# Routing tokens of three chunks inside the attention stream, into fixed slot regions per expert

## What is computed

```python
scores = x_flat @ gate_w + gate_b                       # (2048, 8)
topk_vals, topk_idx = jax.lax.top_k(scores, TOP_K)      # TOP_K = 2
topk_probs = jax.nn.softmax(topk_vals, axis=-1)
combine_w = zeros((T, N_EXPERTS)).at[tok, topk_idx].add(topk_probs)
h = relu(einsum('td,edf->etf', x_flat, w1) + b1[:, None, :])
y = einsum('etf,efd->etd', h, w2) + b2[:, None, :]
out = einsum('te,etd->td', combine_w, y)
x = _layernorm(x + out)
```

## Time and profile before

| | us |
|---|---|
| median of 3 runs | 3154.45 (3149.6 to 3155.65) |
| the profiled execution | 3158.21 |
| its span | 3156.4 |
| TensorE busy, share of the span | 2783.8 (88%) |
| VectorE busy | 2059.6 (65%) |
| ACT busy | 1566.9 (50%) |
| POOL busy | 267.7 (8%) |

### The profile page before, as it was taken

The page is one execution under the profiler, slowest core; times in us unless marked ns, Lnnn a source line. Parts: engine busy times, 40 slices in busy tenths (PEclk is TensorE's granted clock), DMA queues, the critical chain, the costliest instruction groups (busy, mean ns, idle before and its releaser), DMA issues. The chain is left out here.

```text
span 3156.4 us, 85067 instructions
## 1 busy us (share of the span) xinstructions
PE 2783.8 (88%) x35706; PEld 1409.0 (45%) x35707; DVE 2059.6 (65%) x4240; ACT 1566.9 (50%) x2122; POOL 267.7 (8%) x381
## 2 busy tenths in 40 slices
PE   6796978999986988799999999999999999379992
PEld 3574643444443553244344443433333333246661
DVE  4444138888843236688899898989999995412224
ACT  2232213666662222266777776766676778023331
POOL 2113011000010001300000000000000000210003
PEclk9897988999997998699999999999999999589996
DMA  5412032011001004221211221111111110711112
GB/s 157 120 44 94 0 106 79 20 22 39 3 2 37 1 12 131 74 61 45 57 43 41 62 52 37 45 45 55 45 44 45 45 45 2 260 45 32 32 33 88
DMA packets 114940, 173.56 MB, mean 55 GB/s; under 512 B 19946, under 2 KB 90491, under 8 KB 114211
## 3 DMA queue, kind: packets, MB, share of 16 engines
q1 hardware_dynamic: 108772, 160.02, 17.7%
q0 software_dynamic: 5824, 8.49, 0.9%
HBM read 127.63 MB, written 40.51 MB: 53 GB/s over the span
## 5 line engine op out<-in xcount | busy, mean ns | idle before, releaser
L1307 DVE TENSOR_REDUCE d_part_max<-d_ps_m 128x1 f32<-128x512 f32 (+1 forms) x1964 | 1126.9, 630 | 91.0 <-PE d_ps_m L1294 56.7
L1622 ACT ACTIVATE d_prob<-d_ps_s 128x1024 f32<-128x1024 f32 x928 | 898.6, 1021 | 342.8 <-PE d_ps_s L1484 336.3
L1294 PE MATMUL d_ps_m<-k_st,q_st 97*32 97x512 bf16 (+1 forms) x5296 | 480.9, 361 | 22.2 <-DVE d_part_max L1307 18.0
L1484 PE MATMUL d_ps_s<-q_st,k_st 98*32 98x512 bf16 x5104 | 441.1, 382 | 9.7 <-ACT d_prob L1622 8.3
L698 DVE TENSOR_REDUCE x_part_max<-x_att_ps_m 128x1 f32<-128x512 f32 (+2 forms) x578 | 307.6, 585 | 43.4 <-PE x_att_ps_m L683 17.3
L939 ACT ACTIVATE x_att_prob<-x_att_ps_s 128x1024 f32<-128x1024 f32 (+3 forms) x296 | 258.2, 921 | 131.1 <-PE x_att_ps_s L820 78.1
L1294 PEld LDWEIGHTS d_ps_m<-k_st,q_st 97*32 97x32 bf16 x5296 | 143.5, 96 | 279.5 <-DVE d_part_max L1307 130.5
L1502 PE MATMUL d_ps_o<-d_prob,a_values 128*32 128x512 f32 x2048 | 267.1, 595 | 0.0
L1294 PE MATMUL d_ps_m<-q_st 97*32 97x512 bf16 (+1 forms) x2560 | 231.9, 362 | 2.6 <-DVE d_part_max L1307 0.6
L1484 PEld LDWEIGHTS d_ps_s<-q_st,k_st 98*32 98x32 bf16 x5104 | 138.8, 97 | 187.7 <-issue 74.7
L1502 PE MATMUL d_ps_o<-d_prob,x_values 128*32 128x512 f32 x1664 | 215.4, 593 | 0.4 <-ACT d_prob L1622 0.4
(11 more groups left out here) (328 smaller groups left out, 3336.2 us busy)
## 6 DMA issues: line engine op xcount, KB each, us to landing
k_st<-parts_k SPq DMA_DIRECT2D x90, 256.0 KB, 5.6
k_st<-parts_k SPq DMA_DIRECT2D x90, 208.0 KB, 4.7
l_w<-in_l_w SPq DMA_DIRECT2D x16, 1024.0 KB, 13.4
q_st<-parts_q SPq DMA_DIRECT2D x48, 256.0 KB, 5.0
q_st<-parts_q SPq DMA_DIRECT2D x192, 64.0 KB
q_st<-parts_k SPq DMA_DIRECT2D x30, 256.0 KB
q_st<-parts_k SPq DMA_DIRECT2D x30, 208.0 KB
parts_q<-a_proj_parts SPq DMA_DIRECT2D x16, 384.0 KB, 2.5
```

What stands on the lines that cost most here:

```text
L1294: mm = pe.matmul(bank[q:q + COLUMNS, 0:w], self.query(s, h, ROW_MASK + 1, a * P + q, COLUMNS), self.key(s, h, ROW_MASK + 1, k, w), start=T ...
L1307: dve.tensor_reduce(self.part[:, h * QT + a, i:i + 1], bank[:, 0:w], AX.X, ALU.max).then_inc(s_read, 1)
L1484: mm = pe.matmul(ps_s[u][k:k + COLUMNS, hh, :], maxima.key(s, h, ROW_MAX + 1, kt * P + k, COLUMNS), maxima.query(s, h, ROW_MAX + 1, 0, QC) ...
L1622: act.activation(prob[:, p % 2, 2 * u:2 * u + 2, :], ps_s[u][:, :, :], ACT.Exp, scale=scale).then_inc(s_prob, 1)
```

## The change

- `Plan.close_chunks` hangs three tasks on segment 1's chunks 0 to 2: `gate`, `count` and `scatter`, 14, 17 and 19 pairs behind the chunk's end, that is in the second step of the next chunk. `gate` and `count` use banks of the ring.
- `Router` holds what `route` and `place_tokens` did, for one chunk of four token tiles at a time. Expert e owns the slots from e x 2048 on; a running count `seen` goes from chunk to chunk.
- `dispatch` takes the place of `route` and `place_tokens`. It does the last chunk alone (8 scatters) and makes two tables: each loop pass's expert, and `tile_row`, its tile in the slots.
- `x_slots` has 136 tiles, all cleared; results are stored over the tokens' rows, and `y_slots` is gone.
- SP's loads and stores in `expert_ffn` find their rows by `tile_row`.
- SP loads the biases and two experts in `dispatch`; the other six are issued by POOL at the start of `expert_ffn`.

```diff
+SLOT_TILES = E * NT + E
@@ Plan.close_chunks
+            if si == 1 and c < NQ - 1:
+                self.tasks[start + 14].append(("gate", c))
+                self.tasks[start + 17].append(("count", c))
+                self.tasks[start + 19].append(("scatter", c))
@@ Router
+    def logits(self, pe, c, bank, s_logits):
+        for a in range(QT):
+            for m in range(DT):
+                start = (c * QT + a) * P
+                mm = pe.matmul(bank[:, a * E:(a + 1) * E], self.x_fm[:, m, start:start + P], self.w[:, m, :],
+                               start=(m == 0), stop=(m == DT - 1))
+        mm.then_inc(s_logits, 1)
+    def choose(self, dve, link, c, bank, s_taken, s_gates, n):
...
+        link(*(dve.max(self.best[:, a, :], self.logit[:, a, :]) for a in range(QT)))
+        link(*(dve.max_index(self.index[:, a, :], self.best[:, a, :], self.logit[:, a, :]) for a in range(QT)))
...
+    def counts(self, pe, bank, s_counts):
+        flat = self.gates[:, :, :, :].rearrange("p a s e -> p (a s e)")
+        pe.matmul(bank[:, 0:2 * self.LOGITS], self.ones[:, :], flat, start=True, stop=True)
+        pe.matmul(bank[:, 2 * self.LOGITS:4 * self.LOGITS], self.below[:, :], flat, start=True,
+                  stop=True).then_inc(s_counts, 1)
+    def place(self, dve, link, c, bank, s_ranked, s_slots, n):
...
+        link(dve.tensor_copy(self.total[:, :, :], columns(bank[:, 0:2 * self.LOGITS])))
+        src, side, w = self.total[:, :, :], 0, 1
+        while w < C:
+            dst = self.upto[:, side, :, :]
+            link(dve.tensor_copy(dst[:, 0:w, :], src[:, 0:w, :]),
+                  dve.tensor_tensor(dst[:, w:C, :], src[:, w:C, :], src[:, 0:C - w, :], ALU.add))
+            src, side, w = dst, 1 - side, 2 * w
...
+    def scatter(self, pool, c):
+        for i in range(2 * QT * c, 2 * QT * (c + 1)):
+            pool.indirect_dma_start(self.x_slots, bass.IndirectOffsetOnAxis(self.slots[:, i:i + 1], 0),
+                                    self.x_tok[:, i // 2, :], None).then_inc(self.s_scatter, 16)
@@ dispatch (in place of route and place_tokens)
+            dve.wait_ge(s_logits, 1)
+            router.choose(dve, link, c, ps_logits, s_taken, s_gates, 0)
+            dve.wait_ge(s_counts, 1)
+            router.place(dve, link, c, ps_counts, s_ranked, s_slots, 0)
...
+            link(dve.tensor_copy(tile_row[:, :], row_f[:, :]))
@@ expert_ffn
-        def rows(dram, i):
-            return dram[bass.ds(i * P, P), :]
+        def rows(queue, dram, i):
+            row = queue.value_load(tile_row[0:1, bass.ds(i, 1)], min_val=0, max_val=SLOT_TILES - 1)
+            return dram[bass.ds(row * P, P), :]
...
             def load(i):
-                sp.dma_start(x_rows[:, :], rows(x_slots, i)).then_inc(s_row, 16)
+                sp.dma_start(x_rows[:, :], rows(sp, token_slots, i)).then_inc(s_row, 16)
             def store(i):
                 sp.wait_ge(s_y, i + 2)
-                sp.dma_start(rows(y_slots, i), y_rows[:, :]).then_inc(s_stored, 16)
+                sp.dma_start(rows(sp, token_slots, i), y_rows[:, :]).then_inc(s_stored, 16)
...
             pool.sem_inc(s_y, 1)
             pool.sem_inc(s_stored, 16)
+            load_late(pool)
             for e in range(E):
                 pool.wait_ge(s_expert[e], 32)
                 pool.sem_inc(s_resident, 1)
@@ decoder_kernel
-                         cst["zeros"][:, :].rearrange("p (o n) -> p o n", o=1).to_broadcast((P, EXPERT_TILES, D)))\
+                         cst["zeros"][:, :].rearrange("p (o n) -> p o n", o=1).to_broadcast((P, SLOT_TILES, D)))\
-EARLY_EXPERTS = 3
+EARLY_EXPERTS = 2
```

More of the change, by code:

```diff
@@ L1353, in decoder_attention, with dve_links, link @@
+def dve_links(dve, s_chain):
+    links = 0
+    def link(*made):
+        nonlocal links
+        for instruction in made:
+            instruction.then_inc(s_chain, 1)
+            links += 1
+        dve.wait_ge(s_chain, links)
+    return link
+def decoder_attention(nc, name, plan, maxima, router, q_st, x_tok, x_fm, ctx_fm, t, cst):
     segments = plan.segments
@@ L1392, in decoder_attention @@
         s_store = [sem(f"store{i}") for i in range(2)]
+        s_gate_w, s_const, s_logits, s_taken, s_gates, s_counts, s_ranked, s_slots, s_chain = map(
+            sem, ("gate_w", "const", "logits", "taken", "gates", "counts", "ranked", "slots", "chain"))
         block = ctx.enter_context(nc.Block())
@@ L1568, in unit_product, with gate_logits, gate_counts @@
                 mm.then_inc(s_mm, 1)
+            def gate_logits(step):
+                c = step[1]
+                pe.wait_ge(s_gate_w, 32)
+                pe.wait_ge(s_xfm, QT * (NQ + c + 1))
+                bank_free(step)
+                router.logits(pe, c, plan.bank(step), s_logits)
+            def gate_counts(step):
+                pe.wait_ge(s_const, router.CONSTANTS)
+                pe.wait_ge(s_gates, 2 * (step[1] + 1))
+                bank_free(step)
+                router.counts(pe, plan.bank(step), s_counts)
             def v_product(step):
@@ L1606, in _ @@
                         v_product(task)
+                    elif task[0] == "gate":
+                        gate_logits(task)
+                    elif task[0] == "count":
+                        gate_counts(task)
         @block.scalar
@@ L1809, in _ @@
                         add_value_bias(task)
+                    elif task[0] == "gate":
+                        choose(task)
+                    elif task[0] == "count":
+                        place_chunk(task)
 def gelu_ffn(nc, name, x_tok, z_tok, x_fm, w1, b1, w2, b2, cst):
@@ L2228, in _ @@
         def _(sp):
-            load_more(sp)
+            load_early(sp)
         @block.tensor
         def _(pe):
[L2234 to L2237, removed]
+            router.logits(pe, c, ps_logits, s_logits)
+            pe.wait_ge(s_gates, 2)
+            router.counts(pe, ps_counts, s_counts)
         @block.vector
         def _(dve):
[L2241 to L2247, removed]
+            link = dve_links(dve, s_chain)
             link(dve.memset(ladder[:, 0:1], 0.0))
@@ L2302, in _ @@
[L2302 to L2313 removed]
+            pool.wait_ge(s_slots, 1)
+            router.scatter(pool, c)
+EARLY_EXPERTS = 2
@@ L2367, in expert_ffn @@
         s_resident = sem("resident")
-        s_part, s_first, s_sum, s_out = map(sem, ("part", "first", "sum", "out"))
+        s_top, s_part, s_first, s_sum, s_out = map(sem, ("top", "part", "first", "sum", "out"))
         s_two = [sem(f"two{i}") for i in range(DEPTH)]
```

214 lines of the change are left out of this document (136 added, 78 removed).

## The result

| kernel | chips | median us | ratio to the kernel before, 95% interval |
|---|---|---|---|
| changed | kind B (first comparison) | 3202.5 | 1.0154 [1.014, 1.0168] |
| changed, unaltered, again | kind B | 3203.6 | 1.016 [1.0143, 1.0177] |
| changed, unaltered, again | kind A | 3172.5 | 1.0074 [1.0054, 1.0094] |

The change makes the kernel slower, by less than 2% but clear of the noise. By how much depends on the chip, or on what else went with it, which the experiments brought to light: in two comparisons it was 1.5 to 1.6%, in a third 0.7%. I call the two sorts kind B and kind A; the kernel before takes 3154 to 3155 us on B and 3149 to 3151 us on A.

What follows compares the result with a forecast made beforehand. Bounds: a stream with TensorE 96% and VectorE 90% busy, a bare routing and scatter chain, the expert loop's ring. Sum -28.9+36.4+0.6+21.6+2+1 = +32.7 on 3154.5 gave 3187 us; range 3150 to 3225.

Steps and rivals of the forecast that it cites:

- The shorter gap: Between stream and experts: only 4 of 16 token tiles remain to dispatch, first product at 2727.1 instead of 2782.26, 55.2 us won.
- The hold: Start of the experts: first product waits until POOL has issued twelve 1 MB weight loads, 30 us (10 to 76).
- (a): Rival at the experts' start: POOL issues large loads as fast as small ones, 10 us; sum +12.7, 3167 us; chance 0.17.
- Contention: First expert tiles: late weights still flow while these tiles load their rows, 1 us (0 to 4).
- The loop: Expert loop: two table reads on SP cost 1.2 us (0.57 to 1.4), 0.19 slack; 36 loads, 36.4 us (14 to 44).
- Rival (c): Expert loop: table reads overlap SP's other work, period stays 7.98; 3150 us, or 3130 with POOL's issues at 10; chance 0.12.
- The stream: Joint attention stream: routing the other 12 token tiles adds 7.2 us for each of three chunks, 21.6 (8 to 28); scatters free.
- The clearing: Before the GELU block: clearing 136 tiles instead of 39 lasts 51 us and delays the GELU weights 2 us (0 to 8).

Runs made afterwards that it cites:

- The spaced loads: Changed kernel with POOL issuing the twelve late expert loads one behind each of the first twelve turned tiles, not all at once: 3190.8 against 3203.6 us unaltered, kind B.

## Why the prediction was right and where it was wrong

The forecast (3187, slower with 0.80) named the direction, and the range held the medians of both kinds of chip. Its steps:

- **The shorter gap: right, with two small errors that cancel.** -55.2 us forecast from step 31 to the first product, ahead of the hold; -55.2 and -55.7 measured. The chain of choosing, placing and eight scatters was priced from the short steps of the earlier trace rows and the scatters of the earlier trace rows. It was 1.7 us shorter than that, and the first product came 1.6 us later behind its load than before, which is contention.
- **The hold: failed.** 30 us forecast, none measured. Two things went wrong. A large load was priced near SP's 2.1 us, but POOL is not paced by transfers: it issued one each 0.82 us, the low bound, while they took 18.5 to 29.2 us to land. And the step took POOL's issues as standing ahead of its semaphore increment, while its sequencer had announced weights with six issues still to come. Of the rivals (a) came nearest, but even its 10 us were not there. The Trainium skill (DMA: Bandwidth & Descriptors, Anatomy of one DMA — SWDGE (gpsimd) path) calls the generation of descriptors small. The trace agrees, 1024 rows costing 0.2 us more to issue than 256.
- **Contention: failed.** 1 us forecast (0 to 4), 4.8 + 8.5 = 13.3 measured in the stretches from the first product on; 1.4 of the 8.5 are the reads of the loop, and the 1.6 of the first landing come on top, so 13.5. The step took the late weights to hinder the first tiles only a little, since the hold would have kept most of them apart; without a hold, 12.6 MB and the first loads of `x_rows` start in the same microsecond. The spaced loads gave 12.8 back.
- **The loop: right mechanism, undersized.** 36.4 forecast for 36 periods at 9.0, 47.9 measured, 35 periods longer by 1.37. The mis-sized term is the pair of reads. They cost 0.68 (bias add to store) and 0.74 us (store to load), 1.42 instead of 1.2, just over the upper bound. Against this, load issue to transpose gave 0.32 us back (2.09 instead of 2.41) where 0.19 was counted as slack; and TensorE, which now stands idle ahead of the transpose, needs 4.32 us from there to the bias add instead of 4.08. For the turn shown that is 1.42 - 0.32 + 0.24 = 1.34. The bare table load took 0.28 us, as ACT's did; the rest of what a read adds is register steps and the address. The Trainium skill (DMA: Bandwidth & Descriptors, Latency and other measured facts) gives a floor of about 600 ns for a tensor load. The rows show 0.26 to 0.36 us for it on SP, and the measurement decides. Rival (c), the fast side, fell: the reads were hidden only when the code was made to hide them.
- **The stream: right on kind A, failed on kind B.** 21.6 forecast, 18.8 measured on kind A (three steps at 6.3 longer than before), and 46.7 on kind B, where the sentence that POOL's scatters cost nothing failed, as far as the loss begins beside them; that they are its cause is not shown. The forecast's own terms add up to 7.05 a step, not 7.2, which changes nothing. No row of the profile before shows indirect DMAs beside a full stream, which the step should have said: POOL's scatters stood there only in the gap, where the other engines were waiting anyway.
- **The clearing: failed, harmlessly.** 2 us forecast, 0 measured; its low bound held.

The total came nearer than its terms. On kind B the hold put 26 us too many into the sum (30, less the 3.7 that the first product needs anyway), against 25 too few in the stream, 12 in the contention and 12 in the loop. On kind A, where the stream's term held, the hold (26 too many) and the other two (10 and 11 too few) nearly cancel. That is luck, not accuracy.

## What to carry to other kernels

A dynamic address costs its read where the read stands: put it ahead of the wait, not behind, and a ring without slack gives all of it back. When transfers move from a queue that paced them to one that doesn't, look at what else begins in that microsecond; spacing them by need cost a few lines. Work that is to vanish in a full stream needs a stretch where an engine really has nothing to do, and its price there should be measured on more than one chip.

## What the runs showed of the hardware

- **The same program can cost 9 us more a step on another chip, beside POOL's indirect DMAs.** On kind B a step with a group of eight takes 53 us, on kind A 44, and on A the group costs nothing (44.0 with it and 43.9 without any, on one chip). The tail with its 32 gathers on POOL differs too: in the changed kernel it lasts 55.4 us on B and 52.0 on A, although the gathers start over the same 39.4 and 39.3 us; what is longer is the work behind the last one, 12.9 against 9.6. The kernel before has a tail of 56.5 us in its one profile, and its median is some 4 us higher on B. Whether it is the chip, the place in memory or other work on the chip is open.
- **TensorE's granted clock falls behind the loss.** TensorE was busy 7.05 of 12 us beside the scatters of kind B, then the granted clock was 0.51 for 10 us; on kind A it was busy 11.56 of 12 and stayed at 1.00.
- **POOL's sequencer runs ahead of the DMA issues queued to it**, here by six loads; an increment written behind twelve issues came when the seventh had just begun, 4.9 us after the first.
- **A load of 1 MB on POOL takes 0.73 to 0.98 us to issue**, no more than an indirect scatter of 128 KB (0.97 to 1.23).
- **Twelve such loads at once stretch a small load's landing from 2.0 to 6.6 us** until they are through.
